# Layer 0 attention: score matmuls from 16-bit parts of the rotated q and k

## The reference, cut to what matters

```
q = rope(y @ Wq);  k = rope(y @ Wk);  v = y @ Wv;  g = sigmoid(y @ Wg)
s_cmp  = q . mean of k over each block of 64 positions, masked   -> p_cmp, o_cmp
s_full = q . k * scale                     (512 x 512, causal)
p_slc  = softmax(where(causal, s_full))         # 8 blocks of 8 are selected: all
p_swa  = softmax(where(causal and distance <= 64, s_full))
o = o_cmp * g_cmp + o_slc * g_slc + o_swa * g_swa ;  x + o @ Wo
```

## Time and profile before

| what | value |
|---|---|
| median of three runs | 2533.44 us |
| profiled execution, its span | 2525.72 us, 2524.0 us |
| layer 0 attention heads, first to last score matmul | 95.5 to 1342.7 us |
| busy over the whole span | TensorE 83%, VectorE 70%, ScalarE 54%, GpSimd 44% |
| mean granted TensorE clock | 0.922 of full |

### The profile page before, as it was taken

One profiled execution on the slowest core, in us unless ns is written; L12 is line 12 of the kernel. 1 busy time (PEld: TensorE's weight loads), 2 busy tenths in 40 slices (PEclk: granted clock), 3 DMA queues, 4 the chain that ended last, 5 costly groups with the idle time before them and its releaser, 6 DMA issues. The chain is left out here.

```text
span 2524.0 us, 43575 instructions
## 1 busy us (share of the span) xinstructions
PE 2093.1 (83%) x14585; PEld 1307.1 (52%) x14585; DVE 1767.6 (70%) x3446; ACT 1355.4 (54%) x3223; POOL 1101.9 (44%) x759
## 2 busy tenths in 40 slices
PE   0678888999999999999995669956789898966999
PEld 0355555565565565566663635533456666643444
DVE  7788877888888878887663449844567767754770
ACT  4566655555555555655553524315476767646442
POOL 5566646555565555554442046633232223210440
PEclk9989988999999999999998579987689899988999
DMA  4233223222122212221122864445333333337110
GB/s 164 80 99 94 80 81 110 76 74 77 60 83 89 70 59 72 78 93 59 56 64 85 334 248 144 144 170 159 102 126 114 102 120 102 118 112 257 34 46 21
DMA packets 112540, 268.53 MB, mean 106 GB/s; under 512 B 10752, under 2 KB 40832, under 8 KB 109824
## 3 DMA queue, kind: packets, MB, share of 16 engines
q1 hardware_dynamic: 93264, 217.50, 25.5%
q10 hardware_dynamic: 16560, 40.64, 4.9%
q0 software_dynamic: 2560, 8.39, 0.9%
HBM read 182.60 MB, written 76.55 MB: 103 GB/s over the span
## 5 line engine op out<-in xcount | busy, mean ns | idle before, releaser
L830 PE MATMUL ps_q<-a_y,a_w 128*128 128x512 f16 x1536 | 356.8, 382 | 0.0
L616 POOL TENSOR_TENSOR a_rb<-a_rb,a_rot 128x512 f32<-128x512 f32 x129 | 187.5, 1454 | 309.0 <-ACT a_rb L729 309.0
L830 PEld LDWEIGHTS ps_q<-a_y,a_w 128*128 128x128 f16 x1536 | 149.8, 102 | 163.8 <-issue 6.1
L620 POOL TENSOR_TENSOR a_qk<-a_ra,a_rb 128x512 f32<-128x512 f32 x129 | 204.6, 1586 | 18.9 <-POOL a_rb L616 0.5
L257 DVE TENSOR_TENSOR_SCAN wkv_bwd<-wk_decay,wkv_tail,wkv_fwd 128x512 f32<-128x512 f32 x114 | 198.5, 1763 | 0.1
L880 PE MATMUL ps_g<-a_o,a_wo 128*128 (+1 forms) x768 | 177.8, 381 | 13.3 <-POOL a_o L607 10.7
L847 PE MATMUL ps_s<-a_qk 128*128 128x512 f32 (+3 forms) x512 | 173.2, 460 | 15.3 <-POOL a_qk L620 15.3
L839 PEld LDWEIGHTS ps_v<-a_w,a_y 128*128 128x128 f16 x3072 | 176.9, 98 | 15.1
L869 PE MATMUL ps_o<-a_tt_,a_v 128*128 128x512 f32 (+3 forms) x512 | 174.6, 488 | 11.1 <-ACT a_tt_ L747 9.5
L839 PE MATMUL ps_v<-a_w,a_y 128*128 128x128 f16 x3072 | 182.0, 219 | 0.0
L968 DVE TENSOR_REDUCE a_nmax<-ps_s 128x1 f32<-128x512 f32 (+3 forms) x256 | 124.7, 487 | 72.1 <-PE ps_s L849 65.4
(11 more groups left out here) (271 smaller groups left out, 4938.6 us busy)
## 6 DMA issues: line engine op xcount, KB each, us to landing
a_w<-wqkv_split SPq DMA_DIRECT2D x48, 768.0 KB, 4.7
scratch_numlog<-wkv_nl ACTq DMA_DIRECT2D x40, 512.0 KB, 2.9
wkv_kt<-in_fT ACTq DMA_DIRECT2D x59, 256.0 KB, 2.7
a_wraw<-in_wqkv SPq DMA_DIRECT2D x18, 768.0 KB, 5.4
wqkv_split<-a_w SPq DMA_DIRECT2D x17, 768.0 KB, 6.8
a_stacks<-qk_parts SPq DMA_DIRECT2D x102, 128.0 KB
gate_up<-in_gate_up SPq DMA_DIRECT2D x8, 1408.0 KB, 14.2
a_nlc<-scratch_numlog SPq DMA_DIRECT2D x18, 512.0 KB, 4.5
```

What stands on the lines that cost most here:

```text
L616: pool.tensor_tensor(rb[:, n, :], rb[:, n, :], rot[:, 2 * n + 1, :], ALU.mult).then_inc(s["roped"], 1)
L620: pool.tensor_tensor(qk[:, n, :], ra[:, n, :], rb[:, n, :], ALU.add).then_inc(s["q_sb"], 1)
L830: mm = pe.matmul(psq[n][:], w16[:, i % 2, wp, n, c, :], y16[:, yp, c, :], start=c + m == 0, stop=c == CC - 1 and m == 2)
```

## The change

Layer 0's scores are no longer one 32-bit matmul per tile, but three 16-bit ones: q and k are each split into a high part (rounded to 16 bits) and a low part (the rest), and high x high, high x low and low x high are summed in PSUM. The mask matmul stays. ScalarE makes both high parts (`high`), GpSimd makes q's low part, VectorE k's low part. q's high part is made right behind `swap(g, 1)`; k's behind the three copies of the former head's transposed P. The block scores (L821) and the block sums of k (L960) still use the 32-bit `qk`.

```diff
+        qk16 = sb("qk16", [P, 2, 2, T], F16)
 # GpSimd, group
                         rope(g, 1)
+                        pool.wait_ge(s["q_hi"], g + 1)
+                        pool.tensor_tensor(qk16[:, 0, 1], qk[:, 0, :], qk16[:, 0, 0], ALU.subtract).then_inc(s["q_lo"], 1)
 # ScalarE
+                def high(g, n):
+                    act.wait_ge(s["q_sb"], g * 2 + n + 1)
+                    if not (isinstance(g, int) and g == 0):
+                        act.wait_ge(s["scores"], g * 3)
+                    act.activation(qk16[:, n, 0], qk[:, n, :], ACT.Copy).then_inc(s["k_hi" if n else "q_hi"], 1)
-                def turn(g, group, i):
+                def turn(g, group, i, ahead=True):
                     for m in range(3):
                         ...
                         act.activation(tt_[:, m, 0:w], ps[m][:, 0:w], ACT.Copy).then_inc(s["t_sb"], 1)
+                    if ahead:
+                        high(g + 1, 1)
                     act.wait_ge(s["pv"], g + 1)
 # ScalarE, group
                         swap(g, 1)
+                        high(g, 0)
                         act.wait_ge(s["vproj"], g + 1)
                         ...
+                        if not (i or output_before or not first):
+                            high(g, 1)
 # TensorE
                 def scores(g):
-                    pe.wait_ge(s["q_sb"], g * 2 + 2)
+                    pe.wait_ge(s["q_lo"], g + 1)
+                    pe.wait_ge(s["k_lo"], g + 1)
                     for bank, tiles in BANK_TILES:
                         for j in tiles:
-                            pe.matmul(cols(ps, j), qk[:, 0, j * P:(j + 1) * P], qk[:, 1, 0:P * (j + 1)],
-                                      start=True, stop=False)
+                            for m, (qp, kp) in enumerate(PARTS):
+                                pe.matmul(cols(ps, j), qk16[:, 0, qp, j * P:(j + 1) * P], qk16[:, 1, kp, 0:P * (j + 1)],
+                                          start=m == 0, stop=False)
 # VectorE, group
                         sum_keys(g)
+                        dve.wait_ge(s["k_hi"], g + 1)
+                        dve.tensor_tensor(qk16[:, 1, 1], qk[:, 1, :], qk16[:, 1, 0], ALU.subtract).then_inc(s["k_lo"], 1)
                         softmax(b, g, c * G + i, between)
```

More of the change, by code:

```diff
@@ L399, in layer0_attn @@
             "x_loaded", "sig_step", "sig", "lsum", "inv", "yf", "yhi", "ylo", "y_here", "gates_raw", "gates_step",
-            "gates_sig", "gates", "qproj", "cosed", "swapped", "roped", "q_sb", "ksum", "vproj", "v_sb", "scores",
+            "gates_sig", "gates", "qproj", "cosed", "swapped", "roped", "q_sb", "q_hi", "k_hi", "q_lo", "k_lo", "ksum", "vproj", "v_sb", "scores",
             "cmp_ps", "nmax", "sc", "expd", "cmp_step", "cmp_e", "coef", "p_step", "p", "turned", "t_sb", "pv", "of", "o_hi", "o_lo",
@@ L795, in _ @@
                 swap(0, 0)
-                run(act, group, lambda: turn(B * H0 - 1, (B * CC - 1) % 2, G - 1))
+                run(act, group, lambda: turn(B * H0 - 1, (B * CC - 1) % 2, G - 1, False))
                 for slot in range(1, PER):
```

## The result

The changed kernel takes 2634.03 us in the median (2628.83 to 2637.88, four runs), the kernel before 2533.38 beside it. The ratio is 1.0416, with a 95% interval from 1.0395 to 1.0436: 4.2% slower. The profiled execution took 2637.83 us for a span of 2636.1, at a mean granted clock of 0.905.

What follows compares the result with a forecast made beforehand. Two about equally long chains, TensorE's and VectorE's, were taken to bound the kernel head by head. Middle 57, last batch 9, first batch 7 and clock 10 gave +83 us: 2616 us in the median, range 2558 to 2675.

Steps and rivals of the forecast that it cites:

- The reversal of sign: Middle stretch: TensorE looks like the bound, but VectorE's chain is as long, so cheaper scores lose; slower had chance 0.92.
- The saving: Scores on TensorE: three 16-bit matmuls per tile plus masks take 1.93 us instead of 2.55, 0.62 us less a head.
- The collision for i = 1 and 3: VectorE's subtraction for k's low part waits out GpSimd's L196; scores start 1.9 us later for i = 3, same pattern for i = 1.
- i = 2: Middle stretch: late block sums hold up k's low part, +1.9 us, or +3.8 with L276 and L603 colliding; +2.4 taken.
- i = 3 and the clock: Middle stretch, i = 3: k's low part behind L196, +1.3 us; clock falling behind new gaps, 0.8 us in 12 groups, +10.
- i = 0: Middle stretch: second scan and o_low delay the low parts, +3.3 us, or +0.8 where VectorE gets by; +2.5 taken.
- i = 1: Middle stretch: k's low part waits behind GpSimd, partly offset by output matmuls no longer waiting for o_low; +0.9 us.
- The sum for the middle: Batches 1 and 2: 7.1 us a group over eight groups, +57 us, bounds +22 to +78, clock loss counted separately.
- The last batch: Last batch's heads: low part fits for i = 1, about +1.3 us each for i = 2 and 3; +9 in all.
- ScalarE's copies: Two added copies making the high parts of q and k, 0.63 us, nearly free since ScalarE is busy 57%.
- The signs: Trace: TensorE waits 2 to 3.9 us for i = 0 and 2, VectorE idles over 1 us, scores take 1.9 us a head.
- The second rival: Whole kernel: clock falls behind most gaps and places reach upper bounds, +143 us at worst, +115 taken, 2648 us; chance 0.20.

Runs made afterwards that it cites:

- the first experiment: Against the changed kernel, VectorE makes k's low part ahead of the block sums of k, not behind them; 2579.11 us.

## Why the prediction was right, and where its sizes were off

**The reversal of sign** (TensorE 94% busy, and yet cheaper matmuls lose) rested on VectorE's block sums ending at or behind the start of the scores. The experiments bear it out: without the wait the ratio is 1.0065, with it 1.0416.

**The saving**, 0.62 us a head: measured 0.60 by the 32-bit version with all waits, give or take 0.15. Right.

**The collision for i = 1 and 3**: forecast +1.9 us, scores 7.3 us behind the start of the scans; the trace has 7.30, and the run with the wkv sums moved shows that the delay came from GpSimd. Right, though it was a race that looked even; L196 won it in all 16 heads of the middle stretch.

**i = 2** was sized too low: +2.4 us was taken between 1.9 and 3.8, and the trace has +3.7. Both collisions that make up the upper bound happen; I had given more weight to L276 getting ahead of q's low part, but they start 0.02 us apart and L276 takes 1.72 us.

**i = 3 and the clock**: +1.3 was forecast and +3.0 measured. The difference is the clock, the term of the sum that was mis-sized most: behind the gap of 4.6 to 4.9 us at i = 2 six of the eight heads of the middle stretch start their scores on the lower level and two fall to it within the first three matmuls, which costs 2.0 us in the step to i = 3 (20.47 against 18.51 and 18.49 with the gap filled, which is +1.0 against the kernel before). I had 10 us for the clock in all, and 16 came in the middle stretch alone.

**i = 0** was sized too high, +2.5 against +1.9, i = 1 too low, +0.9 against +1.3. The sum for the middle was 57 with the clock apart, some 64 with its share; 79 were measured. The last batch came as forecast (+9; from the trace +8.9), the first at +11 instead of +7. Together the heads lost 99 us from first to last scores, and every part but i = 0 and the last batch was taken too low.

**ScalarE's copies** were taken as free. In the changed kernel they are nearly so. VectorE waits for ScalarE before k's low part in four heads of the last batch (0.67 to 1.06 us) and one of the first; but without the low parts' waits, the next wait in line is k's high part (26.6 us), and in the version with q's parts early they were on the path.

**The signs** that the prediction named came in part. VectorE's idle time before the maxima is 1.4 us a head, and L1066 takes 0.68 to 1.63 us. But the gaps of "2 to 3.9 us for i = 0 and 2" are 4.6 to 4.9 for i = 2 and at most 2.3 for i = 0 but for one of 3.7, i = 1 and 3 have some 1.7 each, and scores of 1.9 us a head hold for i = 1 and 3 but not for i = 2 (3.1 to 3.6). The second rival's sum doesn't add up from the prediction's own bounds either: with +20 and +25 for the last and the first batch in place of 15 and 10 it would be +163 at the worst, not +143.

What stays: 16 us (1.0065 to 1) in the version that waits for no low part. It has the full saving of about 40 us, so the added load and the wait for the high parts must cost some 56 us. How this divides between VectorE's 0.68 to 1.63 us ahead of the maxima, and GpSimd's and ScalarE's share, was not taken apart.

## What to carry to other kernels

When an engine at 94% gets less work, look for the second chain before counting the gain: work of VectorE that TensorE now has to wait for costs its own time, the time of what stands ahead of it in VectorE's stream, and whatever it collides with. Where instructions of two engines hold each other up, as k's low part and L196 did here (1.62 against 0.68 us), the place of an instruction in the other engine's stream is part of its price; three times here, moving one collision brought up the next. A saving of 0.6 us a head didn't pay for a hand-over through three engines whose input is ready at the last moment. And when a gap moves, the clock moves with it: read it head by head, not from the mean.

## What the runs showed of the hardware

An instruction of VectorE with two SBUF inputs (L1066), 0.68 us alone, took 1.62 beside a GpSimd instruction of 1.25 us that had started 0.2 us earlier, and again 0.68 when that instruction was moved. Where about 0.5 us of the GpSimd instruction was left, it took less: 1.00 us in the first experiment, 1.05 with y's low part late.

The length of a gap of TensorE doesn't by itself tell the clock behind it. Behind gaps of 1.67 us for i = 1 and 3 of the middle stretch all scores of the changed kernel ran at full speed (1.85 us). Behind 2.94 us (no low part of q) seven of eight heads started at half speed, behind 3.34 us (k's low part first) two of eight, behind 4.06 to 4.30 us (y's low part late) four of eight, behind 4.6 to 4.9 us (the changed kernel) six of eight. What else decides was not taken apart. Filling 3.4 of the 4.9 us kept the clock up in all eight heads, in both runs that did it.
